# A scratch clearing taken out behind every pair of gathers, and all pieces written out in a new order

## The chip, the cores and the metric

One core of one Trainium2 chip runs the whole program. The metric is the device time of one execution in microseconds, lower is better. A run's times are given as the median of repeated executions; the profile comes from one more execution, which has a time of its own.

## What is computed

The input is a batch of 16 images of 64 channels and 128 x 128 pixels, and 128 text tokens per image. For each image, 1024 query points on a 32 x 32 grid are sampled, each predicts 8 offsets, and the feature map is sampled bilinearly at the 8 displaced points. Attention over these 8 points gives 1024 tokens, to which the text tokens are joined (1152 tokens, 64 channels). Then follow one recurrent-style layer and a feed-forward layer of 16 experts, of which each token uses two, computed densely.

```python
q_feat = bilinear_sample(feature_map, ref[:, :, None, :])[:, :, 0]
h = gelu(layer_norm(q_feat @ W_o1 + b_o1, ln_g, ln_b))
off = (h @ W_o2 + b_o2).reshape(B, Nq, 8, 2) * 4.0
sampled = bilinear_sample(feature_map, ref[:, :, None, :] + off * scale)   # B,1024,8,64
keys, values = sampled @ W_k.T, sampled @ W_v.T
attn = softmax(einsum('bnhd,bnphd->bnhp', q, k) / sqrt(8))
h = concatenate([einsum('bnhp,bnphd->bnhd', attn, v).reshape(B, Nq, 64), txt], axis=1)
h = h + lru(layernorm(h)) 
...
hidden = silu(einsum('bsd,edh->bseh', x, w1)) * einsum('bsd,edh->bseh', x, w2)
expert_out = einsum('bseh,eho->bseo', hidden, w3)
return h + einsum('bseo,bse->bso', expert_out, dispatch)
```

## The kernel before

Each engine runs one program, and every hand-over between engines is a semaphore. Nothing sorts the work at run time: for each engine a string in `ORDER` gives the order of its pieces for all 16 images, one letter per piece (`KINDS` translates), and the function `pieces` walks it. An engine works strictly in the order of its string, so a piece that waits holds up all that stands behind it. Pieces of three or four images are interleaved: while the experts of image b run, the attention of image b+1 is made, and the map of image b+2 is loaded and turned.

The pieces of one image, in the order in which they depend on one another:

- `A1` (`a`, 16 times): SP loads eight rows of the map (`L`, letter `p`) into `xin`; PE turns four of them into `bank_a` (L715), ACT copies them to `pixmaj` (L839). After every fourth, SP stores a quarter of the turned map to the table in memory (`Q`, letter `A`, L507 to L517).
- `A2`, `A3`, `B0` to `B6` (`b` to `j`): query features, queries and offsets. `B1` (`e`) is a layer norm: DVE makes a variance, POOL raises it to the power -1/2 (L589), DVE goes on in `B2` (`f`). `B6` (`j`) gives the indices `idx` (L1133).
- `G` (`o`, 32 times, POOL, L560 to L581): two gathers (one per neighbour point, 128 rows of 1 KB each) into `gath`, and behind them `RESTS` clearings of the scratch row `rest`, which nobody reads. `gath` has two buffers of one tile (eight points) each, and each is taken in two halves, so a half needs two `G` and there is room for four halves.
- `D1` (`k`, 16 times, DVE, L1053): one half times its four bilinear weights, into `wsam`. `D2` (`l`): PE adds and turns it (L693). `D3` (`m`): PE makes keys and values (L703), ACT copies them out (L820, L824), DVE multiplies keys with queries (L1059). `D5` (`n`) sums, `S1` to `S3` (`B`, `C`, `D`) are the softmax and the weighted sum, once for each half image.
- for each of three token groups: `P1` to `P8` (`r` to `z`) layer norms, recurrence and gate. Two of them have a POOL part too, a power -1/2 (L594): `P1` (`r`) and `P5` (`v`).
- for each group and each of 16 experts: `X` (`G` in the strings of PE, ACT and DVE), `W` (`F`, PE) and `Z` (`H`, DVE). One `X` is called a slot here: 48 slots per image, 768 in all. They give the strings a ruler: a piece stands at slot s when s `X` stand ahead of it. In steady state, image b has its own attention in 48 slots, counted here from its first `D1`.

POOL's string thus holds only `o`, `e`, `r` and `v`: gathers, with three kinds of small powers between them. For image 7 its part reads `eoovoooooorooooovoooooroooooovoooooooro` (the other steady images differ from it by a pair moved across one `v` or `r`): two pairs of gathers still belong to the image before (its indices are older), then a `v`, after which the new indices are used; 29 pairs lie between them and the `r` that ends the image, one more behind it.

```python
                for n in range(RESTS * (4 * QT * b + k), RESTS * (4 * QT * b + k + 1)):
                    wait(pool, rested, n)
                    nc.gpsimd.memset(rest[:], 0.0).then_inc(rested, 1)
```

Of the kernel before, what the change touches and what calls it, by code (L numbers as in the profile page):

```python
# [77 lines left out]
def grid():  # L78
# [84 lines left out]
        "GFaGlFamGFsmGtFaGlFaGFuFGalGFmbbmGFbbGbFbwbGFblGFylGFcGmFGmFdGFlGFelGFmGFsmGtFGlFGFluhGiFmGFmGFaaGFw",
        "GaFaGFyFGaGFaGaaFGFGFlGFGFlsGFtmGFmGFulGFGlFaGFmGFmwGFlGFylGFGmFaGmFaGFlGFaGFlaGmFsmGtFaGlFaGFuFaGbl",
        "GFmbmGFbbGbFbwbGFblGFylGFcGmFGmFdGFlGFelGFmGFsmGtFGlFGFuhGliFmGFmGFaaGFwGaFaGFyFGaGFaGaaFGFGFlGFGFls",
        "GFtmGFmGFulGFGlFaGFmGFmwGFlGFylGFGmFaGmFaGFlGFaGFalGFmsGmtFaGlFaGFuFaGbblGFmGFmbbGbFbwbGFblGFylGFcGm",
        "FGmFdGFlGFelGFmGFsmGtFGlFGFuhGiFlGFmGFmaaGFwGaFaGFyFGaGFaGaaFGFGFlGFGFlsGFtmGFmGFulGFGlFaGFmGFmwGFlG",
        "FylGFGmFaGmFaGFlGFaGFaGlFsmGtmFaGlFaGFuFaGbblGFmGFmbbGbFbwbGFblGFylGFcGmFGmFdGFlGFelGFmGFsmGtFGlFGFu",
        "hGilFGmFGmFaaGFwGaFaGFyFGaGFaGaaFGFGFlGFGFlsGFtmGFmGFulGFGlFaGFmGFmwGFlGFylGFGmFaGmFaGFlGFaGFalGFmsG",
        "mtFaGlFaGFuFaGblGFmbmGFbbGbFbwbGFblGFylGFcGmFGmFdGFlGFelGFmGFsmGtFGlFGFuhGiFlGFmGFmaaGFwGaFaGFyFGaaG",  # L170
        "FaGaFGFGFlGFGFlsGFtmGFmGFulGFGlFaGFmGFmwGFlGFylGFGmFaGmFaGFlGFaGFaGlFsmGtmFaGlFaGFuFaGbblGFmGFmbbGbF",
        "bwbGFblGFylGFcGmFGmFdGFlGFelGFmGFsmGtFGlFGFuhGliFmGFmGFaaGFwGaFGFyaFGaaGFGaaFGFGFlGFGFlsGFtmGFmGFulG",
        "FGlFaGFmGFmwGFlGFylGFGmFaGmFaGFlGFaGFalGFmsGmtFaGlFaGFuFaGblGFmbGmFbbGbFbwbGFblGFylGFcGmFGmFdGFlGFel",
        "GFmGFsmGtFGlFGFuhGiFlGFmGFmaaGFwGaFaGFyFGaGFaGaaFGFGFlGFGFlsGFtmGFmGFulGFGlFaGFmGFmwGFlGFylGFGmFaGmF",
        "aGFlGFaGFlaGmFsmGtFaGlFaGFuFaGblGFmbmGFbbGbFbwbGFblGFylGFcGmFGmFdGFlGFelGFmGFsmGtFGlFGFuGlhFGimFGmFa",
        "aGFwGFaGFyFGaaGFaGaFaGFGFlGFGFlsGFtmGFmGFulGFGlFaGFmGFmwGFlGFylGFGmFaGmFaGFlGFaGFaGFlsGmtmFaGlFaGFuF",
        "aGbblGFmGFmbbGbFbwbGFblGFylGFcGmFGmFdGFlGFelGFmGFsmGtFGlFGFuhGilFGmFGmFaaGFwGaFGFyaFGaaGFGaaFGFGFlGF",
# [1025 lines left out]
```

## Time and profile before

| | |
|---|---|
| median of 3 runs | 2320.62 us (2315.28 to 2321.72) |
| profiled execution | 2306.16 us, its span 2304.3 us |
| mean granted TensorE clock | 0.949 of full speed |
| PE, DVE, ACT, POOL busy | 2034.4, 1995.7, 941.8, 1690.9 us |
| gathers on POOL | 1024, mean 1111 ns |
| clearings on POOL | 1024, mean 422 ns |

The span is the time from the first to the last instruction; the other 1.9 us lie around it. Busy times leave out waits on semaphores and the issuing overhead between instructions, so an engine can be full without being busy for the whole span.

### The profile page before, as it was taken

Reading aid. Unit: us, or ns where it says so; the run is one execution under the profiler, and the core shown is the slowest. Engines: PE = TensorE matmul, PEld = TensorE weight load, DVE = VectorE, ACT = ScalarE, POOL = GpSimd, SP = SyncE. Lnnn points to the kernel's source line nnn. Section 1 sums busy time; section 2 is a strip of 40 time slices with the busy share of each in tenths; the row PEclk is TensorE's granted clock in tenths of the full one; section 3 lists DMA queues with packets and bytes.
Section 4 is the critical chain, followed back from the end, with each engine's and each line's share of the span. In section 5 each row is a group of like instructions: output and inputs, shape, how many; then the busy total and the mean of one; then the engine's idle time right before and its main releaser. Section 6 shows DMA issues by size and latency. Waiting matters only on the chain.

```text
span 2304.3 us, 46464 instructions
## 1 busy us (share of the span) xinstructions
PE 2034.4 (88%) x15249; PEld 1842.3 (80%) x15249; DVE 1995.7 (87%) x6209; ACT 941.8 (41%) x2040; POOL 1690.9 (73%) x2169
## 2 busy tenths in 40 slices
PE   2468889989899998989999998999999899998889
PEld 1357678888888888888888888888888788888788
DVE  1247899899989999998999999998999999899988
ACT  1224334444444344444434444443444444343333
POOL 0478787888787887878788787878778787878810
PEclk9768999999999999999999999999999999998989
DMA  8766626566553665656455666636466663632200
GB/s 204 219 198 174 180 78 186 158 181 182 141 167 111 174 174 167 183 162 173 112 169 153 169 182 168 177 91 192 135 171 182 169 178 110 178 110 71 69 16 6
DMA packets 363149, 346.84 MB, mean 151 GB/s; under 512 B 49312, under 2 KB 313632, under 8 KB 362784
## 3 DMA queue, kind: packets, MB, share of 16 engines
q1 hardware_dynamic: 313760, 209.59, 33.5%
q0 software_dynamic: 49152, 134.28, 19.7%
q8 instruction: 124, 2.03, 0.4%
q14 instruction: 113, 0.93, 0.1%
HBM read 205.89 MB, written 137.89 MB: 149 GB/s over the span
## 4 chain that ended last, share of the span: by engine, by line
PE 40%; DVE 27%; POOL 17%; issue 11%; DMA 4%; ACT 1%; DVEq 0%; SPq 0%; POOLq 0%
POOL gath L574 11%; PE bank_o L637 10%; PE bank_h L628 6%; PE bank_d L693 6%; PE bank_h L629 6%; PE bank_d L703 5%; DVE ob L975 5%; POOL rest L581 4%; DVE wsam L1053 4%; DMA gath<-table,idx 4%; DVE hid L964 3%; DVE v_sb L1088 2%; DVE v_sb L1081 2%; PE bank_a L715 1%; DVE k_sb L1059 1%
## 5 line engine op out<-in xcount | busy, mean ns | idle before, releaser
L574 POOL DMA_INDIRECT gath<-table,idx x1024 | 1137.7, 1111 | 268.4 <-issue 238.9
L637 PEld LDWEIGHTS bank_o<-w_sb,hid 128*128 128x128 f32 x4608 | 629.8, 197 | 68.7 <-issue 60.7
L637 PE MATMUL bank_o<-w_sb,hid 128*128 128x64 f32 x4608 | 626.4, 274 | 30.4 <-DVE ob L975 29.9
L628 PE MATMUL bank_h<-xsplit,w 128*128 128x384 f32 x1536 | 611.8, 398 | 37.7 <-DVE hid L964 35.5
L787 ACT ACTIVATE silu<-bank_h 128x384 f32<-128x384 f32 x768 | 380.3, 495 | 439.2 <-PE bank_h L629 431.5
L629 PE MATMUL bank_h<-xsplit,w 128*128 128x384 f32 x1536 | 530.3, 345 | 0.0
L975 DVE SCALAR_TENSOR_TENSOR ob<-bank_o,disp,ob 128x64 f32<-128x64 f32 x2160 | 475.4, 275 | 4.8 <-PE bank_o L637 4.4
L581 POOL MEMSET rest<- 1x400 f32 x1024 | 432.3, 422 | 29.6
L964 DVE TENSOR_TENSOR hid<-silu,bank_h 128x384 f32<-128x384 f32 x768 | 420.0, 547 | 25.7 <-ACT silu L787 20.5
L693 PE MATMUL bank_d<-eye,wsam 128*128 128x128 f32 x2048 | 295.1, 291 | 83.8 <-DVE wsam L1053 82.4
L1053 DVE TENSOR_TENSOR wsam<-gath,cw 128x1024 f32<-128x1024 f32 x256 | 311.8, 1218 | 60.6 <-DMA gath<-table,idx 52.1
L628 PEld LDWEIGHTS bank_h<-xsplit,w 128*128 128x128 f32 x1536 | 301.4, 196 | 60.1 <-DVE hid L964 31.1
L693 PEld LDWEIGHTS bank_d<-eye,wsam 128*128 128x128 f32 x2048 | 247.0, 152 | 105.1 <-DVE wsam L1053 101.5
L629 PEld LDWEIGHTS bank_h<-xsplit,w 128*128 128x128 f32 x1536 | 302.1, 197 | 2.8
L703 PE MATMUL bank_d<-w_kv,samT 128*128 128x256 f32 x1024 | 283.2, 400 | 9.3 <-ACT v_sb L824 5.2
L715 PE MATMUL bank_a<-eye,xin 128*128 128x128 f32 x1024 | 174.1, 297 | 86.0 <-DMA xin<-x_dram 39.8
L594 POOL TENSOR_TENSOR lns<-lns,neghalf 128x3 f32<-128x3 f32 x96 | 94.2, 982 | 191.7 <-DVE lns L943 191.4
L839 ACT COPY pixmaj<-bank_a 128x512 f32<-128x512 f32 x256 | 150.2, 587 | 201.2 <-PE bank_a L715 201.0
L715 PEld LDWEIGHTS bank_a<-eye,xin 128*128 128x128 f32 x1024 | 130.6, 159 | 109.5 <-issue 57.9
L703 PEld LDWEIGHTS bank_d<-w_kv,samT 128*128 128x128 f32 x1024 | 184.9, 196 | 41.4 <-issue 18.3
L820 ACT COPY k_sb<-bank_d 128x256 f32<-128x256 f32 x256 | 95.4, 373 | 243.2 <-PE bank_d L703 243.2
L1059 DVE TENSOR_TENSOR k_sb<-k_sb,q_sb 128x256 f32<-128x256 f32 x256 | 107.0, 418 | 89.2 <-ACT v_sb L824 89.1
(142 smaller groups left out, 1865.5 us busy)
## 6 DMA issues: line engine op xcount, KB each, us to landing
table<-pixmaj SPq DMA_DIRECT2D x80, 1024.0 KB, 12.1
xin<-x_dram SPq DMA_DIRECT2D x256, 256.0 KB
table<-pixmaj SPq DMA_DIRECT2D x32, 960.0 KB, 8.5
table<-pixmaj SPq DMA_DIRECT2D x16, 1088.0 KB
gath<-table,idx POOLq DMA_INDIRECT x1024
out_dram<-ob SPq DMA_DIRECT2D x48, 96.0 KB
gath<-w_dram SPq DMA_DIRECT2D x4, 512.0 KB, 8.7
interp_sb<-interp_dram SPq DMA_DIRECT2D x1, 1024.0 KB, 5.6
```

The lines of the kernel that those rows point to most:

```text
L574: pool.indirect_dma_start(out=gath[buf][:, p, :, :].rearrange("p a c -> p (a c)"), out_offset=None, in_=table[par], in_offset=bass.Indirec ...
L581: nc.gpsimd.memset(rest[:], 0.0).then_inc(rested, 1)
L628: mm(bank[:, 0:GC], w12[:, e, which, 0, :], xsplit[gp][:], start=True, stop=False)
L629: mm(bank[:, 0:GC], w12[:, e, which, 1, :], xsplit[gp][:], start=False, stop=True).then_inc(ready, 1)
L637: last = mm(bank_o[n % 2][:, C * k:C * (k + 1)], hid[:, n % HB, 128 * k:128 * (k + 1)], w3_sb[:, e, :], start=True, stop=True)
L693: last = mm(bank_d[:, 128 * (2 * f + pair):128 * (2 * f + pair + 1)], wsam[:, corner, 2 * pair:2 * pair + 2, :].rearrange("p n c -> p (n c)"),
L703: last = mm(bank_d[:, 256 * i:256 * (i + 1)], samT[:, 2 * f + i, :], w_kv[:], start=True, stop=True)
L715: last = mm(bank_a[:, 128 * r:128 * (r + 1)], xin[u % 2][:, HW * (4 * (c % 2) + r):HW * (4 * (c % 2) + r + 1)], eye[:], start=True, stop=T ...
L787: nc.scalar.activation(silu[e % 2][:], bank_h[r][:, 0:GC], ACT.Silu).then_inc(silu_done, 1)
L964: tt(hid[:, n % HB, :], silu[e % 2][:], bank_h[r][:, 0:GC], ALU.mult).then_inc(hid_done, 1)
L975: stt(ob[gp][:, k, :], bank_o[n % 2][:, C * k:C * (k + 1)], disp[gp][:, k, e:e + 1], (ob[gp] if e else h2[g])[:, k, :], ALU.mult, ALU.add) ...
L1053: tt(wsam[:].rearrange("p a n c -> p n a c"), gath[j % GB][:, 4 * f:4 * f + 4, :, :], spread(w, 3, C), ALU.mult).then_inc(weighted, 1)
```

## The change

`RESTS` goes from 2 to 1: behind each pair of gathers stands one clearing of `rest`. All five strings of `ORDER` are written anew; each holds the same letters as often as before, so no other instruction is added or removed. The core of the diff:

```diff
 GB = 2
-RESTS = 2
+RESTS = 1
 HB = 4
...
     "pe": (
-        "aaaaaaaaaaaaaaaabbbbbbbbcdehiaaaaaaaallmmalaaalmmlalamamabbblbbbbblcmdmelhilmamaalalasmatmualaaawaly",
+        "aaaaaaaaaaaaaaaabbbbbbbbcdehiaaaaaaaallmmlaaalammllmamalaabbbbbbbblcmdmellmhmilalsamtmualaaalwmyGmaG",
...
     "dve": (
-        "efhjkkmmnkkmmnkkmmnkkmmeknfBhkCjmDmknrkstmkmunvxkwyGmzGkmGnHGHGHGHGkHGHGHGHmGkmHnGBHGHHCkDGrmkmsntGH",
+        "efhjkkmkmnkmkmnkmkmnkmkmenBfkChDmmknrjkstkmmunvkxwymkmznGGGHkGHGHGHmGHkmGnHBGHGHCkDkrmmGsntHkGHGHuvm",
...
     "pool": (
-        "eoooooooooooooooooooeoooooorooovooooooooooorooovooorooeoovooooooooroooovoooooooooorooovoooorooooovoo",
-        "ooooorooeooovoooooooorooooovoooooroooooovoooooorooeovoooooorooooovoooooroooooovoooooooroeoovoooooorooooo",
+        "eooooooooooooooooooooeoooooroooovooooooooooorooovoooorooooovooooooooorooeovoooooooroooooovoooooorooo",
+        "oooovoooooorevoooooooroooooovoooooorooooooovoooooorevoooooooroooooovoooooorooooooovoooooorevooooooor",
...
     "sp": (
-        "ppEEppAppAppAppAppAppAppAppAppppppAAAppAqEqpqpAppAppAqpEpAqppAppAqppAqppAEqppAppAqppAqppAEqppAppAqpp",
+        "ppEEppAppAppAppAppAppAppAppAppppAAppAppAqEqppAppAqppApqpAEqppAppAqppAqppAEqppAppAqppAqppAEqppAppAqpp",
```

From image 3 on POOL's part for one image becomes `evoooooooroooooovoooooorooooooovoooooor`: no gather stands between `r`, `e` and `v` any more, all 32 pairs of an image stand between its first `v` and the last `r`. On DVE the steady string keeps its shape; the 16 `D1` of an image stand at slots 0, 2, 4, 7, 10, 12, 15, 16, 20, 22, 26, 28, 31, 32, 36, 37 (before: 0, 2, 4, 7, 9, 12, 15, 18, 21, 22, 26, 28, 31, 33, 36, 38), and `B6`, which gives the indices, keeps its place 8 slots ahead of the first of them. In the first image the `D1` and `D3` of neighbouring tiles are interleaved on DVE (`kmkmn` for `kkmmn`).

## Rows read from the trace of the kernel before

**Rows 1.** The page: span, and the chain that ended last, by line.
```profile
span 2304.3 us, 46464 instructions
...
POOL gath L574 11%; PE bank_o L637 10%; PE bank_h L628 6%; PE bank_d L693 6%; PE bank_h L629 6%; PE bank_d L703 5%; DVE ob L975 5%; POOL rest L581 4%; DVE wsam L1053 4%; DMA gath<-table,idx 4%; DVE hid L964 3%; DVE v_sb L1088 2%; DVE v_sb L1081 2%; PE bank_a L715 1%; DVE k_sb L1059 1%
```

**Rows 2.** Windows: length, PE, PEld, DVE, ACT, POOL busy, granted clock, DMA share, GB/s.
```profile
90.00:185.00 95.00, 59.97 (x357) 45.57 (x356) 37.95 (x69) 22.92 (x50) 76.51 (x102) 0.61 0.74 209
185.00:457.00 272.00, 240.47 (x1785) 215.09 (x1784) 232.41 (x704) 112.88 (x243) 218.71 (x283) 0.95 0.56 157
722.00:1922.00 1200.00, 1111.62 (x8566) 1015.01 (x8564) 1109.14 (x3466) 523.75 (x1142) 956.41 (x1213) 0.97 0.57 161
2201.00:2304.00 103.00, 92.20 (x621) 87.81 (x619) 89.50 (x334) 34.77 (x72) 3.40 (x4) 0.93 0.02 5
```

**Rows 3.** Timeline of POOL: the power of `B1` of images 3 and 15.
```profile
456.21 1.66 POOL L589 TENSOR_TENSOR off_s<-off_s,neghalf 128x8 f32<-128x8 f32 x1
...
2056.66 1.71 POOL L589 TENSOR_TENSOR off_s<-off_s,neghalf 128x8 f32<-128x8 f32 x1
```

**Rows 4.** Timeline of POOL, one steady period (image 7).
```profile
1005.92 1.07 POOL L574 DMA_INDIRECT gath<-table,idx  x1 [1.80 <-DVE idx L1133]
...
1075.68 0.95 POOL L574 DMA_INDIRECT gath<-table,idx  x1 [0.16 <-issue]
1076.93 0.95 POOL L574 DMA_INDIRECT gath<-table,idx  x1 [0.30 <-issue]
1077.88 0.90 POOL L581 MEMSET rest<- 1x400 f32 x2
1078.94 2.00 POOL L574 DMA_INDIRECT gath<-table,idx  x1 [0.16 <-issue]
...
1117.33 0.89 POOL L594 TENSOR_TENSOR lns<-lns,neghalf 128x3 f32<-128x3 f32 x1
```

**Rows 5.** The chain that ended last, in order of time: two clearings in that period.
```profile
1071.00 0.43 POOL rest L581
...
1071.48 0.42 POOL rest L581
```

**Rows 6.** By line: durations of all instructions in ns, minimum/median/maximum.
```profile
L574 POOL DMA_INDIRECT gath<-table,idx x1024: 942/960/3035, 89.7 to 2196.3; - x171
...
L581 POOL MEMSET rest<- x1024: 421/422/447, 92.1 to 2197.8; 1x400 f32 x171
...
L1053 DVE TENSOR_TENSOR wsam<-gath,cw x256: 1204/1216/1293, 98.8 to 2201.6; 128x1024 f32<-128x1024 f32 x128
```

**Rows 7.** Who waited for whom, 722 to 1922 us: total, times, longest.
```profile
DVE k_sb L1059 <- ACT v_sb L824: 30.3, 26, 2.4
DVE wsam L1053 <- DMA gath<-table,idx: 24.4, 19, 2.4
...
PE bank_d L693 <- DVE wsam L1053: 36.0, 41, 2.0
...
POOL lns L594 <- DVE lns L943: 76.9, 41, 6.1
```

**Rows 8.** Timeline of DVE, same period as rows 4: two waits for gathers.
```profile
998.77 1.22 DVE L1053 TENSOR_TENSOR wsam<-gath,cw 128x1024 f32<-128x1024 f32 x1 [1.26 <-DMA gath<-table,idx]
...
1078.89 1.23 DVE L1053 TENSOR_TENSOR wsam<-gath,cw 128x1024 f32<-128x1024 f32 x1 [1.22 <-DMA gath<-table,idx]
```

**Rows 9.** Windows, as in rows 2, around the second of those waits.
```profile
1076.00:1084.00 8.00, 8.00 (x54) 6.68 (x53) 6.02 (x15) 5.79 (x13) 6.96 (x9) 1.00 1.06 308
```

**Rows 10.** The chain in the first image: end of one tile, start of the next.
```profile
116.96 0.49 DVE k_sb L1059
...
117.52 0.57 issue
118.08 1.23 DVE wsam L1053
```

**Rows 11.** Waits of DVE from 90 to 185 us, the first image's attention.
```profile
DVE k_sb L1059 <- ACT v_sb L824: 31.0, 8, 8.4
DVE wsam L1053 <- DMA gath<-table,idx: 17.6, 4, 8.3
```

More of the change, by code:

```diff
@@ L163 @@
[L163 to L177, printed above, removed]
@@ new lines @@
+        "aGFmGFmwGFlGFyGlFGmFaGmFaGFlGaFalaGFmGFsmGtFGlFaGFluGFamGFbmbGFbbGbFbbwbGcFdlGFylGFGmFGmFGFlGeFlGFmG",
+        "FsmGtFGlFGuFlGhFmiGFmGFaaaGFwGaFGFyaFGaaGFaGFGFGFlGFGFlsGFtmGFmGFulGFGlFamGFGFmwGFlGFyGlFGmFaGmFaGFl",
+        "GaFalGFmGFsmGtFaGlFaGFluGFamGFbmbGFbbGbFbbwbGcFdlGFylGFGmFGmFGFlGeFlGFmGFsmGtFGlFGuFlGhFimGFmGFaaaGF",
+        "wGaFGFyaFGaaGFaGFGFGFlGFGFlsGFtmGFmGFulGFGlFaGFmGFmwGFlGFylGFGmFaGmFaGFlGFalaGFmGFsmGtFaGlFaGFluGFam",
+        "GFbmbGFbbGbFbbwbGcFdlGFylGFGmFGmFGFlGeFlGFmGFsmGtFGlFGuFlGhFmiGFmGFaaaGFwGaFGFyaFGaaGFaGFGFGFlGFGFls",
@@ new lines @@
+        "GFtmGFmGFulGFGlFaGFmGFmwGFlGFylGFGmFaGmFaGFlGFalaGFmGFsmGtFaGlFaGFluGFamGFbmbGFbbGbFbbwbGcFdlGFylGFG",
+        "mFGmFGFlGeFlGFmGFsmGtFGlFGuFlGhFimGFmGFaaaGFwGaFGFyaFGaaGFaGFGFGFlGFGFlsGFtmGFmGFulGFGlFamGFGFmwGFlG",
+        "FyGlFGmFaGmFaGFlGaFalGFmGFsmGtFaGlFaGFluGFamGFbmbGFbbGbFbbbwGcFdlGFylGFGmFGmFGFlGeFlGFmGFsmGtFGlFGuF",
+        "lGhFimGFmGFaaaGFwGaFGFyaFGaaGFaGFGFGFlGFGFlsGFtmGFmGFulGFGlFaGFmGFmwGFlGFyGlFGmFaGmFaGFlGaFalGFmGFsm",
+        "GtFaGlFaGFluGFamGFbmbGFbbGbFbbwbGcFlGFyGlFGmFGmFdGFlGeFlGFmGFsmGtFGlFGuFlGhFimGFmGFaaaGFwGaFGFyaFGaa",
@@ new lines @@
+        "GFaGFGFGFlGFGFlsGFtmGFmGFulGFGlFamGFGFmwGFlGFyGlFGmFaGmFaGFlGaFalaGFmGFsmGtFGlFaGFluGFamGFbmbGFbbGbF",
+        "bbbwGcFdlGFylGFGmFGmFGFlGeFlGFmGFsmGtFGlFGuFlGhFimGFmGFaaaGFwGaFGFyaFGaaGFaGFGFGFlGFGFlsGFtmGFmGFulG",
+        "FGlFamGFGFmwGFlGFyGlFGmFaGmFaGFlGaFalGFmGFsmGtFaGlFaGFluGFamGFbmbGFbbGbFbbwbGcFdlGFylGFGmFGmFGFlGeFl",
+        "GFmGFsmGtFGlFGuFlGhFimGFmGFaaaGFwaGFGFyaFGaaGFaGFGFGFlGFGFlsGFtmGFmGFulGFGlFaGFmGFmwGFlGFyGlFGmFaGmF",
+        "aGFlGaFalGFmGFsmGtFaGlFaGFluGFamGFbmbGFbbGbFbbwbGcFdlGFyGlFGmFGmFGFlGeFlGFmGFsmGtFGlFGuFlGhFmiGFmGFa",
@@ new lines @@
+        "aaGFwaGFGFyaFGaaGFaGFGFGFlGFGFlsGFtmGFmGFulGFGlFGmFGFmwGFlGFyaGlFGmFaGmFaGFlGaFalaGFmGFsmGtFGlFaGFlu",
+        "GFamGFbmbGFbbGbFbbwbGcFlGFyGlFGmFGmFdGFlGeFlGFmGFsmGtFGlFGuFlGhFimGFmGFaaaGFwGaFGFyaFGaaGFaGFGFGFlGF",
+        "GFlsGFtmGFmGFulGFGlFamGFGFmwGFlGFylGFGmFaGmFaGFlGFalaGFmGFsmGtFaGlFaGFluGFamGFbmbGFbbGbFbbwbGcFdlGFy",
+        "GlFGmFGmFGFlGeFlGFmGFsmGtFGlFGuFlGhFimGFmGFaaaGFwGaFGFyaFGaaGFaGFGFGFlGFGFlsGFtmGFmGFulGFGlFaGFmGFmw",
+        "GFlGFyGlFGmFaGmFaGFlGaFalGFmGFsmGtFaGlFaGFluGFamGFbmbGFbbGbFbbwbGcFdlGFylGFGmFGmFGFlGeFlGFmGFsmGtFGl",
@@ new lines @@
+        "GtmGmGGGlamGGmwGGGlyGmaGmaGGaalGmGsmGtaGBaGlGamGmGGwbGcdGlGyGmGmGGlGmGsmGtGgGlGhmGmGaaaGwGaBGaGaaGya",
+        "GGGGGlsGtmGmGGGlaGmGmwGGlGyGmaGmaGGalaGmGsmGtaGBaGlGamGmGGwbGcdGlGyGmGmGGlGmGsmGtGgGlGhmGmGaaaGwGaBG",
+        "aGaaGyaGGGGGlsGtmGmGGGlaGmGmwGGlGyGmaGmaGGalaGmGsmGtaGBaGlGamGmGGwbGcdGlGyGmGmGGlGmGsmGtGgGlGhmGmGaa",
+        "aGwGaBGaGaaGyaGGGGGlsGtmGmGGGlamGGmwGGGlyGmaGmaGGaalGmGsmGtaGBaGlGamGmGGbwGcdGlGyGmGmGGlGmGsmGtGgGlG",
+        "hmGmGaaaGwGaBGaGaaGyaGGGGGlsGtmGmGGGlaGmGmwGGGlyGmaGmaGGaalGmGsmGtaGBaGlGamGmGGwbGcGGlGymGmdGGlGmGsm",
```

113 lines of the change are left out of this document (51 added, 62 removed).

## Prediction

> **What bounds the kernel now.** I read the shares of the chain that ended last first. No engine owns it: PE and DVE lines carry most, but POOL's gathers hold 11%, the clearings of `rest` 4%, and landings of gathers 4% [rows 1]. So POOL, which does no arithmetic on the tokens, is on the chain, and it has to be seen where.
>
> The windows divide the run. In steady state, 722 to 1922 us, PE is busy for 1111.6 of 1200 us and DVE for 1109.1 [rows 2]: 93 and 92%. The period is read from the power of `B1`, which stands at one place per image: (2056.66 - 456.21) / 12 = 133.37 us for each of the 12 periods between images 3 and 15 [rows 3]. Nine periods lie in the window, so DVE has 10.1 us of idle time in each, PE 9.8. That is all that a re-ordering can give per image; below that both engines would have to do less.
>
> The waits say what the idle time is made of. DVE waited 24.4 us in the nine periods for gathers to land, 2.7 per image, and 30.3 for ACT's copy of the values; PE waited 36.0 us, 4.0 per image, for `wsam`, which stands right behind the landed gathers [rows 7]. POOL waited 76.9 us, 8.5 per image, for the variance of a layer norm, though DVE at other times waits for POOL's gathers: POOL is not short of time over an image, it is late in some stretches and early in others, because of its fixed order.
>
> Next, POOL in one period. Its cycle of a pair is 1075.68 to 1078.94, 3.26 us: two gathers of 0.95, 0.30 between them, two clearings of 0.90 together and 0.16 behind [rows 4]. A half tile needs two pairs, 6.5 us plus what stretches them; DVE wants one about every 38 x 2.78 / 15 = 7.0 us (its 16 `D1` span 38 slots, and a slot is 133.37 / 48 = 2.78 us). With the layer norm powers in the way POOL barely keeps up. Both kinds of lateness are seen: at 1078.89 a `D1` in mid image waited 1.22 us, at 998.77 the last `D1` of the image before waited 1.26 [rows 8]. The last one's gathers are those that stand behind `e` in the string.
>
> **What the change removes.** 512 clearings. Two neighbours start at 1071.00 and 1071.48 [rows 5], so one costs POOL 0.48 us with its issue: 15.4 us per image, 246 us in all, and a pair takes 2.78 us. POOL's own need per image before: 32 x 3.26 = 104.3, plus the stretch of gathers above their median, 64 x (1111 - 960) ns = 9.7 (mean from the table, median from [rows 6]), plus seven powers, six of 0.89 and one of 1.7 us with 0.2 of issue each [rows 3, 4], 8.4: about 122 of 133. After: 89.0 for the pairs, and some 20 more, 109. None of this is saved time in itself: POOL's gain counts only where someone waited for it.
>
> The stretch needs a word. The gather at 1078.94 took 2.00 us; a `D1` of 1.23 us had begun 0.05 us before it [rows 4, 8]. Clearings never stretch (421 to 447 ns), nor does `D1` (1204 to 1293 ns) [rows 6]. Gathers fill 58% of a pair's cycle before (1.90 of 3.26) and 68% after, so if more of them meet a large DVE instruction the stretch grows from 9.7 to some 11.3 us; bounds are 9.7 and, if each of the 16 `D1` blocked POOL for its whole length, 19.5. At that bound POOL needs about 117 of 133 us. The Trainium skill (SBUF — State Buffer, section Who interferes with whom) says that a DVE instruction with two SBUF inputs contends with GpSimd's reads and not with its pure writes, and infers that descriptor generation is spared. The clearings agree, the 2.00 us gather does not; by the page the stretch would stay out and POOL would need 11 us less an image.
>
> **What the new order moves.** On POOL, 29 pairs stood between new indices and the image's last `r`, one between `r` and `e`, two behind `e`. Now all 32 stand ahead of that `r`. From the first gather to `r` took 1117.33 - 1005.92 = 111.4 us for 29 pairs [rows 4]. These were 29 x 3.26 = 94.5, four powers 4.4, stretch 29/32 of 9.7 = 8.8, and 3.7 left for waits. Now: 32 x 2.78 = 89.0, the powers 4.4, stretch 11.3, waits 3.7: 108.4. So `r` and `e` are reached 3 us sooner with three pairs more behind them. At the second `r` after new indices 19 pairs have been issued where 16 had, so the `D1` at 1078.89 has its gathers three pairs, 9.8 us of the old cadence, sooner, and the last half no longer stands behind `e`. Both waits of the period should go. Room in `gath` is not the limit: each pair's buffer is freed by a `D1` four halves ahead, at or before the slot at which POOL gets there.
>
> On DVE some `D1` move by one to three slots, `B6` and the first `D1` keep theirs; on PE and ACT `A1` to `B0` and `D2`, `D3` move by one to four. The instructions are the same, the work beside them is the experts' on both engines (93% full), and I put these moves at nothing; if the cover fails, the price is another wait of 1 to 2 us a piece like those in [rows 7], one per image being 12 to 24 us. SP's string moves a few table quarters and loads in the first two images only by a place or two.
>
> **The sum.** Steady: the 2.7 us of waits for gathers per image. I take 2.2, since in the 8 us around the wait at 1078.89 PE was busy all the time [rows 9]: part of DVE's wait was covered, though PE ran dry later. 12 x 2.2 = 26. Bounds: 0, and the 4.0 us that PE waited for `wsam`, 12 x 4.0 = 48.
>
> Fill: from 90 to 185 us POOL is busy 76.5 of 95 us, DVE only 38.0 [rows 2]. DVE waited 31.0 us for copies and 17.6 for gathers [rows 11]. Its order `kkmmn` makes the next tile's `D1` wait for the last `D3`: 0.49 + 0.57 + 1.23 = 2.3 us on the chain per tile [rows 10]. With `kmkmn` the first of these `D1` lies under PE's and ACT's part, which takes 2.3 us out of some five tiles, 11 us, and the faster pairs (19 x 0.48 = 9 us sooner at the end of them) let the gathers follow. They overlap rather than add; PE's mean granted clock is 0.61 here [rows 2], most of it thus at the 1.2 GHz level, and I leave that as it is. I take 10, bounds 0 and 18.
>
> Drain: after 2201 us POOL has 3.4 us of work [rows 2] and none of it is on the way. The new order ends attention four or five slots sooner, leaving as much expert work behind; 0, give or take 3.
>
> 26 + 10 = 36 us off the profiled execution's 2306.2 us: 2270. The median of the runs lies 14.5 us above that execution; the same 36 us off 2320.6 give 2285 us.
>
> **Rivals.**
> 1. Forecast: waits for gathers go, 2285 us. 0.60, own range 2258 to 2308.
> 2. Hidden anyway. PE and DVE are 93% full and their remaining waits are between themselves (copy of values 3.4 us, `wsam`, `hid`); what DVE no longer waits for gathers it waits for PE some slots later, and the fill is held by PE at its low clock. Gain 0 to 6 us: 2317 us. For it: PE's full window in [rows 9]. Against: PE waited for `wsam` more than DVE for gathers. 0.20.
> 3. Slower: POOL too late for `r`. If a pair does not shrink because the gathers take up the room (a limit behind them that the clearings only covered), 32 pairs of 3.26 us reach `r` 9.8 us later than now; DVE takes `P2` two slots, 5.6 us, behind, so it stands for 4.2 us or more, and with it everything in its string: 12 x 4.2 = 50 us, 2371. It starts to cost at 3.1 us per pair. Against: back-to-back gathers of 0.95 us at a DMA share above 1 [rows 4, 9]. 0.07.
> 4. Slower: the DMA engines. They are at 1.06 in [rows 9]. Gathers 17% closer together take their time from map loads and table stores, and PE stands at `A1`. One such wait of 2 us an image would eat the gain, two give 2310 to 2345. Against: the mean share is 0.57 [rows 2], and among PE's waits of the steady stretch there is none for a load. The Trainium skill (DMA: Bandwidth & Descriptors, section Issuing engines are not separate DMA queues) says that all queues share the same 16 engines and interleave, which is this rival's mechanism. 0.06.
> 5. Slower: the order itself places `D1` or `D3` too early somewhere, 1 to 2 us per image as above without the gain: 2335. 0.07.
>
> **The numbers.** A difference within 0.3% (7 us, 2313.7 to 2327.6) can't be told from no change. Rival 1 is faster (0.60); rival 2 splits, 0.05 faster and 0.15 same; 3 to 5 leave 0.17 slower and 0.03 same. Range: 2255 (48 + 18 us off) to 2326, which takes in rival 2 and leaves out most of 3 to 5.
>
> **What would show it.** Right: no DVE wait for gathers in steady state beyond some 0.5 us per image; POOL's wait for variances up from 8.5 to 20 us or more; gathers that wait for `wsam` (room); a period of about 131.2; pairs at 2.8 us; the power of `B1` of image 3 some 10 us earlier. Wrong: a period of 133 with `k_sb <- v_sb` or PE's waits grown by what the gathers lost (2); `lnx` waiting for POOL (3); PE waiting for `xin` (4); pieces of `D1` waiting for `bank_d` (5).

## The result and the profile after

The changed kernel takes 2247.36 us (2242.19 to 2248.95, 4 runs) beside 2317.95 us (2310.64 to 2321.72, 4 runs) of the kernel before: ratio 0.971, 95% interval 0.9676 to 0.9744. That is 38 us below the predicted 2285 and 8 below the predicted range. On another chip, however, the same kernel took 2488 us (e16); that belongs to the result as much as the 0.971, and the experiments come to it.

The page of the kernel after: span, busy times of all engines, the chain that ended last by engine and by line.

```profile
span 2240.4 us, 45957 instructions
...
PE 2017.2 (90%) x15249; PEld 1837.6 (82%) x15249; DVE 1996.7 (89%) x6209; ACT 942.2 (42%) x2040; POOL 1454.0 (65%) x1657
...
PE 60%; DVE 27%; issue 8%; POOL 2%; DMA 1%; ACT 1%; DVEq 0%; POOLq 0%; ACTq 0%
PE bank_o L637 15%; PE bank_h L628 10%; PE bank_h L629 9%; PE bank_d L693 9%; PE bank_d L703 7%; DVE ob L975 5%; DVE hid L964 4%; DVE wsam L1053 2%; DVE v_sb L1088 2%; PE bank_a L715 2%; PE bank_p L658 2%; POOL gath L574 2%; DVE v_sb L1081 2%; PE bank_p L657 1%; PE bank_p L663 1%
```

POOL's gathers fell from 11% of the chain to 2%, and the clearings have left it [rows 1]. PE is busy for 2017 us and DVE for 1997, 17 us less and 1 us more than before, so of the 63.9 us of span most was idle time of both engines. In steady state, nine periods each way, PE's idle time fell from 88.4 us (1200 less 1111.6, [rows 2]) to 63.5 (1170 less 1106.5).

The timeline of POOL has the powers of `B1` of images 3 and 15, which divide the span as [rows 3] did before.

```profile
433.34 1.63 POOL L589 TENSOR_TENSOR off_s<-off_s,neghalf 128x8 f32<-128x8 f32 x1 [4.41 <-DVE off_s L1104]
...
1994.18 1.63 POOL L589 TENSOR_TENSOR off_s<-off_s,neghalf 128x8 f32<-128x8 f32 x1 [4.70 <-DVE off_s L1104]
```

The period is (1994.18 - 433.34) / 12 = 130.07 us, 3.30 less than 133.37. So the span lost 39.6 us in 12 periods, 22.9 up to image 3, and 1.4 behind image 15 (246.2 us where 247.6 were): 63.9, the whole difference of the spans. Forecast were 26, 10 and 0.

The waits from 692 to 1862 us, nine periods again: total, times, longest.

```profile
DVE k_sb L1059 <- ACT v_sb L824: 18.5, 18, 2.0
DVE hid L964 <- ACT silu L787: 4.0, 6, 1.5
...
PE bank_o L637 <- DVE ob L975: 24.0, 15, 2.5
PE bank_a L715 <- ACT pixmaj L839: 20.1, 27, 0.8
PE bank_h L628 <- DVE hid L964: 11.9, 27, 1.0
PE bank_d L693 <- DVE wsam L1053: 4.7, 9, 0.5
...
POOL lns L594 <- DVE lns L943: 159.1, 31, 13.6
...
POOL gath L574 <- DVE wsam L1053: 1.0, 6, 0.2
```

DVE's waits for gathers (24.4 us) are gone, its waits for the copied values fell from 30.3 to 18.5, and PE's wait for `wsam` from 36.0 to 4.7 us [rows 7]. POOL now waits 17.7 us an image for variances, 8.5 before: it has the time that the clearings left it. Pairs of gathers stand 2.8 us apart, with a clearing of 0.42 us. In image 7 the 18th pair is issued, and the 19th, before the power at 1032.86 that the second `r` of the image asks for, and the ninth `D1`, which needs pairs 17 and 18, finds them landed (timelines of POOL and DVE):

```profile
1025.01 0.95 POOL L574 DMA_INDIRECT gath<-table,idx  x1 [0.31 <-issue]
1025.95 0.42 POOL L581 MEMSET rest<- 1x400 f32 x1
1026.54 0.96 POOL L574 DMA_INDIRECT gath<-table,idx  x1 [0.16 <-issue]
1027.80 0.95 POOL L574 DMA_INDIRECT gath<-table,idx  x1 [0.30 <-issue]
...
1032.86 0.88 POOL L594 TENSOR_TENSOR lns<-lns,neghalf 128x3 f32<-128x3 f32 x1
...
1040.06 1.22 DVE L1053 TENSOR_TENSOR wsam<-gath,cw 128x1024 f32<-128x1024 f32 x1
```

### The profile page after: what moved, and what is told of

It reads as the page before. It is cut to its first block, busy times and chain, and to the rows that moved or that the text cites. A ratio compares the mean times of both kernels' runs of the same rounds, so it can differ in the third digit from the quotient of the medians.

```text
span 2240.4 us, 45957 instructions
## 1 busy us (share of the span) xinstructions
PE 2017.2 (90%) x15249; PEld 1837.6 (82%) x15249; DVE 1996.7 (89%) x6209; ACT 942.2 (42%) x2040; POOL 1454.0 (65%) x1657
## 4 chain that ended last, share of the span: by engine, by line
PE 60%; DVE 27%; issue 8%; POOL 2%; DMA 1%; ACT 1%; DVEq 0%; POOLq 0%; ACTq 0%
PE bank_o L637 15%; PE bank_h L628 10%; PE bank_h L629 9%; PE bank_d L693 9%; PE bank_d L703 7%; DVE ob L975 5%; DVE hid L964 4%; DVE wsam L1053 2%; DVE v_sb L1088 2%; PE bank_a L715 2%; PE bank_p L658 2%; POOL gath L574 2%; DVE v_sb L1081 2%; PE bank_p L657 1%; PE bank_p L663 1%
## 5 line engine op out<-in xcount | busy, mean ns | idle before, releaser
L637 PEld LDWEIGHTS bank_o<-w_sb,hid 128*128 128x128 f32 x4608 | 636.2, 199 | 75.4 <-issue 60.6
L693 PE MATMUL bank_d<-eye,wsam 128*128 128x128 f32 x2048 | 281.8, 283 | 30.1 <-DVE wsam L1053 26.6
L594 POOL TENSOR_TENSOR lns<-lns,neghalf 128x3 f32<-128x3 f32 x96 | 86.2, 898 | 332.0 <-DVE lns L943 330.2
L693 PEld LDWEIGHTS bank_d<-eye,wsam 128*128 128x128 f32 x2048 | 241.9, 148 | 41.3 <-DVE wsam L1053 36.5
L715 PEld LDWEIGHTS bank_a<-eye,xin 128*128 128x128 f32 x1024 | 124.8, 155 | 117.5 <-issue 57.5
L581 POOL MEMSET rest<- 1x400 f32 x512 | 215.9, 422 | 0.2
```

The lines of the kernel that those rows point to most:

```text
L637: last = mm(bank_o[n % 2][:, C * k:C * (k + 1)], hid[:, n % HB, 128 * k:128 * (k + 1)], w3_sb[:, e, :], start=True, stop=True)
L693: last = mm(bank_d[:, 128 * (2 * f + pair):128 * (2 * f + pair + 1)], wsam[:, corner, 2 * pair:2 * pair + 2, :].rearrange("p n c -> p (n c)"),
L715: last = mm(bank_a[:, 128 * r:128 * (r + 1)], xin[u % 2][:, HW * (4 * (c % 2) + r):HW * (4 * (c % 2) + r + 1)], eye[:], start=True, stop=T ...
```

## The experiments

Eighteen kernels ran in five groups, each group on one chip beside the kernel before: e1 to e4 on chip 11, e5 to e8 on chip 0, e9 to e12 on chip 1, e13 to e16 on chip 12, e17 and e18 on chip 4. The kernel before took 2317, 2312, 2315, 2315 and 2311 us there. The chips go by their numbers in the machine; each was used in one group only, so a chip can't be told from its session. Periods below are read from the power of `B1` as above. A kernel's own scatter from one profile to another is known from two pairs: e5 and the kernel after differ by 1.8 us in the time of image 3's `B1` and by 0.2 in the period, e11 and e17 by 7.0 and 0.2.

### First group (chip 11)

**e1**, the kernel before with one clearing:
```diff
-RESTS = 2
+RESTS = 1
```


> The old order with one clearing. Theory POOL (the gain is POOL's time: gathers land earlier, DVE stops waiting for them): two thirds or more of the 64 us of span come with this alone, 2265 to 2280 us, the period falls from 133.4 to some 131, and DVE's waits for gathers in steady state fall below 0.5 us per image. Rival ORDER (the new strings of PE, ACT and DVE save the waits, the clearing only had to make room for them): at most a third, 2300 to 2318 us, the waits for gathers fall but waits of DVE for ACT's copy of the values grow by as much.

Measured: 2452.73 us, ratio 1.0589 (1.0548 to 1.0629).

**e2**, the changed kernel with two clearings:
```diff
-RESTS = 1
+RESTS = 2
```


> The new order with two clearings. Theory POOL: 32 pairs of 3.26 us now stand ahead of the last layer norm power, POOL comes to it 6 to 10 us too late, DVE waits for POOL's powers, and the time is at or above that of the kernel before, 2320 to 2390 us. Rival ORDER: the strings of the other engines keep most of their gain, 2260 to 2300 us.

Measured: 2400.21 us, ratio 1.0359 (1.0328 to 1.039).

**e3**, the changed kernel with none:
```diff
-RESTS = 1
+RESTS = 0
```


> The new order with no clearing at all. Theory POOL: POOL has 25 us or more to spare per image already, so 15 us more change nothing in steady state; only the fill can gain a few us: 2238 to 2248 us. Rival (the clearings pace the DMA engines and some pace is needed): slower than with one clearing by 5 us or more.

Measured: 2787.13 us, ratio 1.2018 (1.1974 to 1.2062).

**e4**, the kernel before with one clearing and POOL's part of an image in the new form:
```diff
-RESTS = 2
+RESTS = 1
...
-roeoovoooooorooooovoooooroooooovooooooo
+revoooooooroooooovoooooorooooooovoooooo
```
(The two lines are one image's part of the string, which repeats.)

> One clearing, the old strings of PE, ACT, DVE and SP, and only POOL's string changed from image 2 on: all 32 pairs ahead of the last power, none behind the power of the offsets, as in the new order. Theory POOL: better than the old order with one clearing by up to 1.3 us per image, since the last half of an image no longer comes late: 2250 to 2270 us. Rival ORDER: the same as the old order with one clearing within 5 us.

Measured: 2453.44 us, ratio 1.0512 (1.0462 to 1.0562).

Only e2 came near a theory, 10 us above the upper end of theory POOL's range. e1, e3 and e4 are slow in a manner that none of my theories had: less work on POOL, and much more time. (e3's rival, that some pace is needed, asked for 5 us or more; 540 came.) Their waits over the whole span name a releaser that the kernel before and the changed kernel don't show at all: `remote`, which stands for an update of the awaited semaphore that the profile can put down to no instruction of this core. From e3, total, times, longest:

```profile
ACT silu L787 <- remote: 201.2, 76, 13.6
DVE ob L975 <- remote: 169.2, 55, 9.2
ACT k_sb L820 <- remote: 119.2, 35, 10.0
ACT pixmaj L839 <- remote: 115.2, 30, 9.5
```

All four wait for a matmul; e16 shows below what such a wait looks like. At this point it was open whether it belongs to the kernel or to the chip.

### Second group (chip 0)

**e5**, the changed kernel, unaltered. 

> The changed kernel once more, beside the kernels below. In the runs with one clearing and the old order, the profile showed waits of up to 4.5 us in which ACT and DVE stood although PE's matmul had ended, 74 times ahead of the silu alone; the kernel before and the changed one had none above 0.04 us. Theory PACE (the new order itself keeps them away): 2247 us within 5, and none of them. Rival CHIP (they come with the chip on which the runs were made): they show here too and the time is above 2300 us.

Measured: 2248.89 us, ratio 0.9722 (0.9688 to 0.9756), and no `remote` wait. That is the number of theory PACE, but this chip shows a `remote` wait in no kernel, so the run doesn't speak for the order.

**e6**, the kernel before with three clearings:
```diff
-RESTS = 2
+RESTS = 3
```


> The old order with three clearings behind each pair. Theory POOL: POOL needs 15 us more per image, 137 of 133, and becomes the bound: 137 to 140 us per period, 2380 to 2450 us, with waits of DVE for gathers of 5 us or more per image. Rival PACE alone (clearings only keep PE's signals prompt, and two do that already): within 10 us of the kernel before.

Measured: 2457.6 us, ratio 1.0617 (1.0584 to 1.065). The period is 143.0 us; DVE waited 79.0 us for gathers in nine of them (24.4 before). At 3.75 us a pair the gathers hold DVE throughout: the mechanism of theory POOL, at more than its 137 to 140 us a period and 8 us above its range.

**e7**, the changed kernel with POOL's part of an image in the old form:
```diff
-revoooooooroooooovoooooorooooooovoooooo
+roeoovoooooorooooovoooooroooooovooooooo
```


> The changed kernel, but POOL's string from image 3 on as before: three pairs of gathers behind the last layer norm power, two of them behind the power of the offsets. Theory POOL: the last half of an image comes late again, DVE waits up to 1.3 us per image for it: 2247 to 2265 us. Rival PACE (the new strings fit each other and any shift brings the late signals of PE back): above 2300 us, with waits for PE that its records do not explain.

Measured: 2330.19 us, ratio 1.0069 (1.0044 to 1.0094). The waits of DVE and POOL from 708 to 1941 us, nine periods of 137.0:

```profile
DVE wsam L1053 <- DMA gath<-table,idx: 50.9, 21, 5.6
...
POOL lns L594 <- DVE lns L943: 250.6, 51, 8.3
```

The same gathers with the same short pairs cost 81 us against e5. Theory POOL had at most 1.3 us an image, for the last half of an image, and missed; rival PACE had the time (above 2300) but not the reason, as there is no `remote` wait. POOL isn't short of time: it waits 27.8 us an image for variances. The waits of DVE don't stand at the last `D1` of an image either (0.2 us in nine periods) but at the ninth (37.0 us of the 50.9) and the tenth (10.1). In the old form only 16 pairs stand ahead of the power of the second `r`, and the ninth `D1` needs pairs 17 and 18 (timelines of POOL and DVE, image 7):

```profile
1060.23 0.88 POOL L594 TENSOR_TENSOR lns<-lns,neghalf 128x3 f32<-128x3 f32 x1 [3.40 <-DVE lns L943]
1061.31 1.78 POOL L574 DMA_INDIRECT gath<-table,idx  x1 [0.20 <-issue]
...
1066.26 0.95 POOL L574 DMA_INDIRECT gath<-table,idx  x1 [0.30 <-issue]
...
1072.22 1.23 DVE L1053 TENSOR_TENSOR wsam<-gath,cw 128x1024 f32<-128x1024 f32 x1 [4.41 <-DMA gath<-table,idx]
```

POOL stands for 3.40 us until DVE has made the variance, issues pairs 17 and 18 only then, and DVE pays for it 4.41 us at the ninth `D1`. In the changed kernel 19 pairs stand ahead of that power, and the wait is gone. This is POOL early and late by turns, as I read it in the kernel before.

**e8**, the kernel before with one clearing as long as two:
```diff
-RESTS = 2
+RESTS = 1
...
-        rest = sb("rest", [1, 400])
+        rest = sb("rest", [1, 856])
```


> The old order with one clearing of 856 elements in place of two of 400: the same POOL time (0.90 us per pair) in one instruction. Theory PACE by time (what matters is how long POOL is off the gathers): 2317 us within 7, no late signals. Rival PACE by count (each clearing with its semaphore wait drains something): near the 2450 us of one short clearing.

Measured: 2312.71 us, ratio 0.9998 (0.998 to 1.0015), period 133.4. One clearing of 802 ns does what two of 422 do, so the number of instructions doesn't count on this chip; as it shows no `remote` wait in any kernel, the two PACE theories aren't decided. One thing in it bears on the account below: the waits for gathers at the last `D1` are nearly gone (0.7 us in nine periods, 10.0 before), PE's wait for `wsam` fell from 36.0 to 26.7 us, and yet the period stayed.

A long clearing has a price of its own, which I had overlooked. DVE's small `TENSOR_SCALAR` instructions, among them the one that makes the variance, run on until a clearing beside them has ended. Its durations in ns, minimum/median/maximum, in e3 (no clearing), the changed kernel (422 ns each), e11 below (1x600) and e8 (802 ns), in this order:

```profile
L943 DVE TENSOR_SCALAR lns<-lns x96: 169/169/171, 185.8 to 2773.1; 128x3 f32<-128x3 f32 x96
L943 DVE TENSOR_SCALAR lns<-lns x96: 168/168/467, 169.3 to 2201.6; 128x3 f32<-128x3 f32 x96
L943 DVE TENSOR_SCALAR lns<-lns x96: 168/170/676, 172.9 to 2240.4; 128x3 f32<-128x3 f32 x96
L943 DVE TENSOR_SCALAR lns<-lns x96: 168/169/878, 181.3 to 2270.0; 128x3 f32<-128x3 f32 x96
```

Summed over all `TENSOR_SCALAR` of a run, the lengthening is about 12 us in the kernel before, 19 in the changed one, 32 in e8 and 38 in e11.

### Third group (chip 1)

**e9**, e1's kernel once more. 

> The kernel before with one clearing of the scratch row in place of two, its order unchanged: the same kernel as e1, once more, on another day of the chip. Two theories of e1's loss. CHIP: the late signals of TensorE (74 waits of ScalarE for a matmul that had long ended, up to 4.5 us each) belong to the chip on which the first four kernels ran; then this run shows none above 0.3 us, DVE's waits for gathers fall from 2.7 us an image to under 1 and the time is 2265 to 2300 us. PACE: they come whenever GpSimd issues its gathers with one short clearing between pairs in the old order; then the time is 2430 to 2470 us again, with waits put down to `remote` or `issue` of 3 us and more on DVE and ACT.

Measured: 2286.0 us, ratio 0.9883 (0.9832 to 0.9934), where e1 had 2452.73. No wait is put down to `remote`. So CHIP holds, though DVE's waits for gathers fell only to 1.5 us an image where it had under 1, and e1 says nothing of what a clearing costs. The waits of e9 from 717 to 1905 us, nine periods of 132.1:

```profile
DVE k_sb L1059 <- ACT v_sb L824: 30.8, 26, 2.4
DVE wsam L1053 <- DMA gath<-table,idx: 13.4, 9, 2.4
...
PE bank_d L693 <- DVE wsam L1053: 25.5, 46, 1.5
```

All 13.4 us stand at the ninth `D1` of an image (13.2 before); at the last one, which had 10.0 us before, nothing is left. The shorter pairs heal what was late because POOL was slow, and not what stands behind a power.

**e10**, the kernel before with one clearing of 600 elements:
```diff
-RESTS = 2
+RESTS = 1
...
-        rest = sb("rest", [1, 400])
+        rest = sb("rest", [1, 600])
```


> The kernel before with one clearing of 600 elements (about 0.6 us) in place of two of 400 (0.84 us): between e1 (0.42 us) and e8 (0.80 us, which left the time where it was). PACE with a threshold: at 0.6 us no late signal yet, and the pairs are 0.2 us shorter, so 2290 to 2312 us. PACE in proportion: some late signals, 2350 to 2400 us. CHIP: 2280 to 2312 us and no late signal, with e9 beside it at 2265 to 2300 us.

Measured: 2296.07 us, ratio 0.9923 (0.9903 to 0.9943); period 132.3, DVE's waits for gathers 12.0 us in nine. In steady state the old order has taken from shorter pairs what it can take already at 0.6 us. CHIP and PACE with a threshold both had this time, and this chip can't part them.

**e11**, the changed kernel with its clearing lengthened:
```diff
-        rest = sb("rest", [1, 400])
+        rest = sb("rest", [1, 600])
```


> The changed kernel with its one clearing lengthened from 400 to 600 elements: 32 pairs an image of some 0.17 us more are 5.4 us of GpSimd's time an image, of the 17.7 us that it waits for the variance in each of the steady images. SLACK: they disappear in that wait, which falls to about 12 us an image, and the time stays at 2240 to 2265 us. DUE TIMES: the order puts its gathers where they come due just as the shorter pairs deliver them, as the 82 us of e7 suggest, and DVE waits for gathers again: 2290 to 2330 us, towards e2's 2400 us at 0.84 us.

Measured: 2278.32 us, ratio 0.9843 (0.9791 to 0.9896), 29 us above e5 on another chip. Neither theory is right as it stood: the time lies between them, near DUE TIMES, yet DVE waits for no gather in the steady stretch. The power of `B1` of image 3 stands at 441.8 us (433.3 in the changed kernel, but 434.8 in e17, the same kernel as this) and the period is 132.1, 2.0 more than in the changed kernel. From the power of image 5 to that of image 14, PE is idle for 0.6 us more an image and busy for 1.2 us more with the same 8577 matmuls, at a mean granted clock of 0.965 where the changed kernel has 0.972; DVE waits 0.5 us for POOL's powers of layer norms, where it waited for none, and its `TENSOR_SCALAR` are held longer by the clearings, as above. Which of these comes first wasn't tested.

**e12**, the kernel before with only DVE's first string changed:
```diff
-        "efhjkkmmnkkmmnkkmmnkkmmeknfBhk...
+        "efhjkkmkmnkmkmnkmkmnkmkmenfBhk...
```


> The kernel before with both clearings, and only DVE's first string changed, from kkmmn to kmkmn in five tiles of image 0, as the new order has it. INTERLEAVE: the weight of each tile reaches GpSimd and PE up to 2.3 us sooner, five times, so that the first image ends up to 11 us sooner: 2300 to 2308 us beside 2312 to 2318 us of the kernel before. HIDDEN: DVE waits for the gathers of the next pair anyway, and the fill gained its 22.9 us after the first image: 2311 to 2319 us.

Measured: 2314.6 us, ratio 1.0006 (0.998 to 1.0032). The waits of DVE from 90 to 185 us, to be held against [rows 11]:

```profile
DVE wsam L1053 <- DMA gath<-table,idx: 31.3, 8, 8.7
DVE k_sb L1059 <- ACT v_sb L824: 21.2, 7, 5.5
```

9.8 us fewer for copies, 13.7 more for gathers: most of the wait changed its name, and HIDDEN holds.

### Fourth group (chip 12)

**e13**, e2's kernel. 

> The changed kernel with two clearings behind each pair, e2 once more. ORDER NEEDS THE SHORT PAIRS (rival 3 the other way round): GpSimd's pairs of 3.3 us don't keep the new order's due times, DVE's squares wait for the variance on GpSimd's queue (5.5 us in e2) and the time is 2370 to 2410 us, with no late signal of TensorE. CHIP: e2 was slow for the same reason as e1, and the new order with two clearings takes 2290 to 2320 us.

**e14**, e3's kernel. 

> The changed kernel without any clearing, e3 once more. CHIP: no late signals; GpSimd has another 13.5 us an image to wait in, and the time is that of the changed kernel or a few us below it, 2235 to 2255 us, since DVE waits for no gather there any more. PACE: gathers without any pause between the pairs hold back something else, and e3's late signals come again: over 2400 us.

**e15**, e12's edit with one clearing. 

> The kernel before with one clearing and kmkmn in five tiles of image 0; e9 (one clearing, order untouched) took 2286 us. INTERLEAVE: with quicker pairs the sooner weights are worth up to 11 us, 2272 to 2280 us. REST OF THE ORDER: nothing, 2282 to 2290 us, as in e12 with two clearings, and the 39 us between e9 and the changed kernel are the order's after image 0.

**e16**, the changed kernel, unaltered. 

> The changed kernel as it stands, as a control beside the other three: 2240 to 2255 us, 0.969 to 0.975 of the kernel before.

Measured: e13 2407.82 us, ratio 1.0372 (1.032 to 1.0424); e14 2784.8, 1.2017 (1.1971 to 1.2064); e15 2466.82, 1.0651 (1.0582 to 1.072); e16 2487.72, 1.0741 (1.0687 to 1.0794). The control is the run that tells most: the very kernel of the 0.971, expected at 2240 to 2255 us, is here 7.4% slower than the kernel before. e13 came as ORDER NEEDS THE SHORT PAIRS had it (2370 to 2410). e14 came as PACE had it (over 2400); its CHIP, which took this chip for one without late signals, missed. e15 is 170 us and more above both of its theories and can't be read for the interleave. The chain of e16 by engine, and its longest waits of this sort:

```profile
PE 58%; DVE 12%; another core or an unknown queue 12%; issue 10%; ACT 5%; DMA 1%; SPq 1%; POOL 1%; DVEq 0%; ACTq 0%; POOLq 0%
```
```profile
ACT pixmaj L839 <- remote: 107.9, 32, 7.3
DVE ob L975 <- remote: 85.7, 54, 5.0
ACT silu L787 <- remote: 55.7, 33, 4.5
```

One core runs, so there is no other one to wait for. One such wait in the timelines of PE, ACT and POOL (start, length; in brackets the idle time ahead and what ended it):

```profile
944.82 0.27 PE L715 MATMUL bank_a<-eye,xin 128*128 128x128 f32 x1
...
947.11 0.34 PE L629 MATMUL bank_h<-xsplit,w 128*128 128x384 f32 x1
953.50 0.87 PE L715 MATMUL bank_a<-eye,xin 128*128 128x128 f32 x3 [6.05 <-ACT pixmaj L839]
...
946.28 0.49 ACT L787 ACTIVATE silu<-bank_h 128x384 f32<-128x384 f32 x1
952.77 0.58 ACT L839 COPY pixmaj<-bank_a 128x512 f32<-128x512 f32 x1 [6.00 <-remote]
...
949.60 0.42 POOL L581 MEMSET rest<- 1x400 f32 x1
950.18 0.95 POOL L574 DMA_INDIRECT gath<-table,idx  x1 [0.16 <-issue]
951.43 2.28 POOL L574 DMA_INDIRECT gath<-table,idx  x1 [0.30 <-issue]
```

PE's matmul into `bank_a` was over at 945.1. ACT was free at 946.8 and began to copy that bank at 952.8, 7.7 us after the matmul; PE, which needed the bank again, stood for 6.05 us. ACT's program has nothing between. As far as the trace tells, what PE signalled reached its reader microseconds late, while POOL went on issuing gathers. The instructions themselves are as long as on the other chips (gathers 1089 ns in the mean where e5 has 1100; clearings 422 in both), so it isn't a slower chip; the mean granted clock is 0.927 for 0.953, with PE idle more.

### Fifth group (chip 4)

**e17**, e11's kernel. 

> The changed kernel with one clearing of 600 elements, e11 once more (2278 us there, without late signals). If this chip shows late signals at all: PACE IN PROPORTION: some of them remain at a pause of 0.6 us, 2330 to 2400 us, between the 2488 us of e16 at 0.42 us and none; THRESHOLD: none, 2270 to 2290 us. If the chip is one without them: 2270 to 2290 us too, and e18 is the run that tells something.

**e18**, e2's kernel. 

> The changed kernel with two clearings. POOL'S QUEUE: its 2400 us come of DVE's and PE's waits for the variance behind the gathers (103 us in e2), which no chip changes, and it takes 2385 to 2410 us here too. CHIP: most of it came of the chips of e2 and e13, and here it takes 2300 to 2350 us.

Measured: e17 2280.31 us, ratio 0.988 (0.9841 to 0.9919), as e11 and as both theories had it for a chip without late signals; e18 2399.26 us, ratio 1.038 (1.0346 to 1.0414). This chip shows no `remote` wait, and e18 still takes what e2 and e13 did: POOL'S QUEUE holds. Its waits from 747 to 2006 us, nine periods of 140.1 (L952 is in `P6`, behind a `v`):

```profile
DVE x2n L952 <- POOL lns L594: 63.1, 14, 5.5
...
PE bank_p L672 <- DVE x2n L952: 49.5, 14, 6.0
```

## Why the prediction was wrong

The sum had 26 us for the steady periods and 10 for the fill; measured were 39.6 and 22.9. Two steps failed: the moves of the order, put at nothing, and the fill term, which went beyond its own upper bound of 18.

From the chips without `remote` waits the two halves of the change can be laid out, as ratios to the kernel before:

| | two clearings | one |
|---|---|---|
| old order | 1 | 0.9883 (e9) |
| new order | 1.038 (e18) | 0.9722 (e5) |

The clearing alone gives 1.2% (0.7 to 1.7), the order alone loses 3.8%, both together gain 2.8%. The halves don't add: the order needs pairs of 2.8 us, and only in that order are such pairs worth more than 1.2%.

**Steady term: right that the waits for gathers go, mis-sized.** The forecast took 2.2 us an image, from DVE's 2.7 us of waits for gathers, and marked it down because PE was full in the 8 us around one of them. Without the discount it would have been 12 x 2.7 = 32; measured were 12 x 3.30. The waits had two causes, which the sum took together. In the kernel before, 10.0 us of the 24.4 stood at the last `D1` of an image and 13.2 at the ninth. Shorter pairs alone (e9) took the first kind and left the second, and the period fell by 1.26. The second kind stands behind the power of the second `r`; it went with the new order, and the period fell by another 2.04. That POOL's string is enough for this wait is seen in e4, which has only that string new: DVE waits for no gather in its steady periods either, though the chip makes its time useless. One window of 8 us was no ground for a discount: as the text itself said, PE ran dry later.

No single wait gives the size. The nine periods from the power of `B1` of image 5 to that of image 14, per image, in us:

| | PE's wait for `wsam` | PE idle | PE busy | period |
|---|---|---|---|---|
| before | 4.0 | 9.8 | 123.8 | 133.6 |
| e8 (old order, one long clearing) | 3.0 | 9.9 | 123.7 | 133.7 |
| e9 (old order, one clearing) | 2.8 | 8.9 | 123.1 | 132.0 |
| after | 0.5 | 7.1 | 123.0 | 130.0 |
| e11 (new order, clearing of 600) | 0.6 | 7.6 | 124.2 | 131.8 |

PE's wait for `wsam`, which I had as the upper bound (4.0 us an image, 48 in all), was nearer the 39.6 than the 26 was, and it follows the period from the kernel before to e9 and on to the changed kernel. That is luck in part: in e8 it fell by 1.0 us and the period stayed, and in e11 it is as low as in the changed kernel and the period is 1.8 us longer. Where it fell without effect, PE was idle elsewhere or busy for longer.

**"Moves at nothing": wrong.** Of the 3.3 us, 2.0 an image come with the order. POOL's own part of it is worth more than that: with the old form of it, and all else new, the period is 137.0 (e7). The prediction had that place too (19 pairs instead of 16 ahead of the second `r`, for the `D1` at 1078.89), and priced it at one wait of 1.22 us. And the moves on the other engines are not nothing either. e7 and e9 have the same clearing and, from image 3 on, the same form on POOL; with the new strings of PE, ACT, DVE and SP the period is 137.0, with the old ones 132.1. The ninth `D1`, which in most images moved from slot 21 to 20, waits 37.0 us in nine periods with the one and 13.4 with the other, 2.6 us an image more; a slot is 2.8. So these moves cost 4.9 us an image with POOL's old form and are part of a gain only with its new one. What POOL's new form is worth with the other strings old stays open, since e4 ran on a chip with late signals; so does which move shortened DVE's waits for the copy, 3.4 to 2.1 us an image. e9 shows that the clearing did not (30.8 us in nine periods).

**Fill term: mis-sized, and the reason given for it fell.** 22.9 us against 10 (bounds 0 to 18). The interleave `kmkmn`, on which most of the 10 rested, is worth nothing by itself (e12). The power of `B1` of image 3 stands at 451.6 us with one clearing in the old order (e9, 4.6 sooner, within what two profiles of one kernel can differ), at 467.8 with the new order and two (e18, 11.6 later), at 433.3 with both. The gain lies behind the first image: from 90 to 185 us the changed kernel's DVE waits 31.5 us for copies and 17.1 for gathers, as before [rows 11], while PE's wait for `wsam` from 185 us up to that power went from 21.3 to 2.8 us. I had looked only at the first image's waits. Which of the moves behind it did this wasn't tried.

**Drain: right** (1.4 us, within the 3 given).

**Rival 3** did not come about, as the pairs did shrink. As a conditional it was right, but for the letter. It said that with pairs of 3.26 us in the new order POOL comes to `r` too late, that DVE stands behind it in `P2`, and 2371 us. e18 has these pairs and 2399 us; DVE waits for POOL's powers 7.5 us an image, of which 7.0 stand in `P6` (L952), behind a `v`, and 0.5 in L949, behind an `r`. **Rival 2** (hidden anyway) fell for the change as a whole; for the interleave alone e12 bears it out. **Rival 4** has next to nothing: in the nine periods PE's matmuls waited 0.9 us for loads of the map, and its weight loads 7.9, which is 0.9 an image (0.2 in all before). **Rival 5** (a `D1` placed too early) shows no wait of its own kind in the changed kernel: DVE waited 2.2 us for `bank_d`. Its mechanism is real, though, and it is what e7 shows, at 4.1 us an image for the ninth `D1`.

**What to look for:** waits for gathers under 0.5 us an image (none), POOL's for variances of 20 us or more (17.7, and 4.7 for `B1`'s, 22.4 together), waits for room (1.0 us in nine periods), pairs at 2.8 us, period 131.2 (130.07), `B1` 10 us earlier (22.9).

**What the prediction had no place for** is the chip. Rival 3 spoke of "a limit behind them that the clearings only covered" and looked for it in the pair itself; on chips 11 and 12 there is one, seen in signals from PE that come late.

## What to carry to other kernels

Sort an engine's late transfers by the piece of work that they stand behind before pricing a faster pace. Those that are late because the engine is slow go with the pace; those that stand behind something it must wait for go only with the order. Give no discount from a single window, and don't price a stall by one named wait, on whichever engine: compare the idle and the busy time of the busiest engine over whole periods. With orders written by hand, a change of a duration and a change of order must be timed together: here the one alone gives 1.2% and the other alone costs 3.8%. An instruction that writes what nobody reads may be a pause that another chip needs: time its removal on several chips beside the old kernel before believing it. On these five, the old order with two clearings was nowhere slow (2311 to 2317 us), and it is the only one timed on all of them.
